# First attention of a four-layer AdaLN/attention/FFN kernel: 16-bit products of ones on TensorE ahead of its waits, and 31 of them in the prologue

## What is computed

```
g  = sigmoid(x) * num / den            # num, den: forward and backward decaying scans of exp(side)
w  = (g @ W.T) as 16 heads of 16       # per sequence
q, k, v = rms(w)*g1, rms(w)*g2, rms(w)*g3
att   = q @ k.T / 4
score = softmax(att, rows) + softmax(att, columns)
x  = x + (score @ v) @ W
```

## Time and profile before

| what | value |
|---|---|
| median of 3 runs | 415.5 us (414.92 to 419.83) |
| the profiled execution, its own time | 418.61 us |
| its span, first to last instruction | 416.8 us |
| mean granted TensorE clock over the span | 0.763 |
| busy: PE, DVE, ACT, POOL | 66%, 71%, 50%, 9% of the span |
| the first attention in this trace | about 36 to 165 us |

### The profile page before, as it was taken

How to read it: one execution, slowest core, us unless ns; L and a number is a source line. 1 busy time by engine, 2 the same in 40 slices (tenths; PEclk the granted TensorE clock), 3 DMA queues, 4 the chain that set the end, 5 groups by cost and what they waited for, 6 DMA issues and landing times.

```text
span 416.8 us, 5215 instructions
## 1 busy us (share of the span) xinstructions
PE 276.7 (66%) x1862; PEld 156.8 (38%) x1867; DVE 296.4 (71%) x536; ACT 208.2 (50%) x422; POOL 39.1 (9%) x61
## 2 busy tenths in 40 slices
PE   0133737548539666637856777979899797975655
PEld 0122314224314224315422245536564454543533
DVE  3998999898798985774598689784436626246861
ACT  5615794865875954352242417415337254332621
POOL 4110120200120113000010100100000000000000
PEclk9999656856957758985785589688658689696985
DMA  7100234445234252005023514391000000000001
GB/s 228 62 0 1 53 68 83 77 76 153 52 69 83 57 102 45 1 1 101 2 50 69 108 31 82 65 267 37 2 0 2 0 2 0 2 0 2 25 25 52
DMA packets 8089, 22.22 MB, mean 53 GB/s; under 512 B 1536, under 2 KB 2944, under 8 KB 7680
## 3 DMA queue, kind: packets, MB, share of 16 engines
q0 software_dynamic: 4032, 14.68, 18.7%
q1 hardware_dynamic: 4032, 7.21, 5.2%
HBM read 6.16 MB, written 1.05 MB: 17 GB/s over the span
## 4 chain that ended last, share of the span: by engine, by line
PE 37%; DVE 36%; issue 11%; ACT 10%; DMA 4%; POOL 0%; DVEq 0%; ACTq 0%; POOLq 0%
DVE fwd L656 5%; PE PS L1222 5%; PE PM L1105 5%; PE PS L1112 4%; PE PO L1238 3%; PE PM L1053 3%; DVE kp L885 3%; PE PM L1175 2%; DVE bwd L662 2%; PE PM L1166 2%; DMA fwd<-mid 2%; DMA fwd<-bwd 2%; ACT E L498 2%; DVE rsum L759 2%; PE PS L1284 2%
## 5 line engine op out<-in xcount | busy, mean ns | idle before, releaser
L885 DVE TENSOR_REDUCE kp<-PS 128x2 f32<-128x256 f32 x64 | 32.3, 550 | 21.0 <-PE PS L1199 20.9
L576 ACT ACTIVATE E<-PS 128x384 f32<-128x384 f32 x64 | 27.8, 488 | 32.7 <-PE PS L1222 32.6
L1112 PE MATMUL PS<-identb 128*128 128x512 bf16 x86 | 33.4, 479 | 16.1 <-ACT E L576 8.4
L498 ACT ACTIVATE E<-PS,negc,escale 128x256 f32<-128x256 f32 x64 | 35.3, 569 | 6.9 <-PE PS L1067 6.9
L1080 PE MATMUL PO<-E,vt 128*32 128x256 f32 x256 | 24.9, 524 | 12.5 <-DVE ytok L787 8.8
L1053 PE MATMUL PM<-ident,kp 128*128 128x128 f32 x128 | 24.4, 353 | 12.9 <-DVE kp L702 7.6
L1088 PE MATMUL PO<-ident,yc 128*128 128x128 f32 x64 | 17.7, 369 | 19.5 <-ACT yc L473 19.5
L490 ACT ACTIVATE E<-PS,negc,escale 128x1024 f32<-128x1024 f32 x16 | 19.2, 1201 | 21.2 <-PE PS L1067 21.2
L1067 PE MATMUL PS<-TP 32*128 32x256 f16 x256 | 21.3, 343 | 9.4 <-DVE TP L714 6.1
L1041 PE MATMUL PM<-w,sg 128*128 128x256 f32 x32 | 12.8, 571 | 21.0 <-DVE sg L689 21.0
L1053 PEld LDWEIGHTS PM<-ident,kp 128*128 128x128 f32 x128 | 19.4, 182 | 18.2 <-issue 9.0
(11 more groups left out here) (179 smaller groups left out, 609.8 us busy)
## 6 DMA issues: line engine op xcount, KB each, us to landing
fwd<-mid POOLq DMA_DIRECT2D x14, 512.0 KB, 4.5
fwd<-bwd POOLq DMA_DIRECT2D x14, 512.0 KB, 4.5
kT<-in_kT SPq DMA_DIRECT2D x4, 256.0 KB, 4.3
xT<-in_xT SPq DMA_DIRECT2D x4, 256.0 KB, 5.8
G<-in_attn SPq DMA_DIRECT2D x1, 1024.0 KB, 4.9
ek<-in_w SPq DMA_DIRECT2D x1, 1024.0 KB, 5.2
ekv<-in_w SPq DMA_DIRECT2D x1, 1024.0 KB, 9.6
out<-mid SPq DMA_DIRECT2D x8, 128.0 KB, 1.7
```

The source lines that it names most:

```text
L498: nc.scalar.activation(E[:, p % 4, i, v * T:(v + 1) * T], PS[:, 2 + i, v * T:(v + 1) * T], ACT.Exp, bias=negc[:], scale=escale[:], accum_o ...
L576: nc.scalar.activation(E[:, p % 4, i, 0:384], PS[:, i, 0:384], ACT.Exp, scale=QSCALE).then_inc(S["e1_done"], 1)
L885: nc.vector.tensor_reduce(kp[:, b % 2, u * H + 2 * j:u * H + 2 * j + 2, D], PS[:, at0:at0 + 2, lo:hi], AX, ALU.max, negate=True).then_inc( ...
L1112: nc.tensor.matmul(bank, identb[:], identb[:, None, :].broadcast_to([P, 4, P]), start=True, stop=True)
```

## The change

`ones` is set to 1.0 at the head of GpSimd's stream, with a semaphore of its own (`ones_set`), instead of behind the two clears of kp. `hot` is a 16-bit view of half of it, and takes the identity's place in all calls of `heat` (those after the first attention too). In the prologue TensorE waits for `ones_set` and for the first scan, and issues 15 products into PS bank 0 ahead of `project0(0)`, 8 behind it, and 8 behind `turn(0)`. In the slots, `warm0(p)` issues one product ahead of `scores0(p)`: at j = 7, and for b >= 1 at j = 0 and 1, into PM bank 0; at j = 2 and 3, for b = 0 also j = 1, for b = 3 also j = 4 and 5, into PM bank 1. That is 4, 5, 5 and 7 products for the four sequences, 21 in all. Each stands behind waits that keep the bank from being overwritten too early, and these now stand ahead of `scores0(p)`.

```diff
+        hot = ones[:, 0:P // 2].bitcast(BF16)
...
+            nc.gpsimd.memset(ones[:], 1.0).then_inc(S["ones_set"], 1)
             nc.gpsimd.memset(lnmin[:], 2.0 ** -60).then_inc(S["ln_bias"], 1)
...
-            nc.gpsimd.memset(ones[:], 1.0).then_inc(S["pads_set"], 1)
             pool.wait_ge(S["gains_done"], 1)
...
-                    nc.tensor.matmul(bank, identb[:], identb[:, None, :].broadcast_to([P, 4, P]), start=True, stop=True)
-
+                    nc.tensor.matmul(bank, hot, hot[:, None, :].broadcast_to([P, 4, P]), start=True, stop=True)
+
+            def warm0(p):
+                b, j = divmod(p, PAIRS)
+                if j == 7 or (j in (0, 1) and b >= 1):
+                    bank = 0
+                    if b < B - 1:
+                        pe.wait_ge(S["qT0_done"], 2 * min(b + 1 + (j == 7), B))
+                    else:
+                        pe.wait_ge(S["qT0_done"], 2 * B)
+                    if p > (B - 1) * PAIRS:
+                        pe.wait_ge(S["w8_done"], 1)
+                elif p > 0 and (j < 4 or (b == B - 1 and j < 6)):
+                    bank = 1
+                    if b >= 2:
+                        pe.wait_ge(S["x_done"], b - 1)
+                else:
+                    return
+                heat(PM[:, bank, :], 1)
+
+            pe.wait_ge(S["ones_set"], 1)
+            pe.wait_ge(S["scan_done"], 1)
+            heat(PS[:, 0, :], 15)
             project0(0)
+            heat(PS[:, 0, :], 8)
             pe.wait_ge(S["ld_ident"], 16)
             turn(0, 0, "ktr0_done", [("k0_done", 1)])
+            heat(PS[:, 0, :], 8)
             for p in range(SLOTS0):
                 b, j = divmod(p, PAIRS)
                 if p < B * PAIRS:
+                    warm0(p)
                     scores0(p)
...
-                    pe.wait_ge(S["pads_set"], 4)
+                    pe.wait_ge(S["ones_set"], 1)
```

More of the change, by code:

```diff
@@ L57 @@
     "gains_done", "ln_bias","qk0_done", "e0_done", "sums_done", "pv0_done", "y0_done", "ytr0_done", "yT0_done",
-    "out0_done", "vcols_done", "rows0_done", "turned0_done",
+    "out0_done", "vcols_done", "ones_set", "rows0_done", "turned0_done",
     "amax_done", "w8max_done", "w8bc_done", "w8_done", "xmax_done", "xbc_done", "xq8_done", "ffn0_done", "y8_done",
```

## The result

| kernel | median, us | against before | 95% interval |
|---|---|---|---|
| changed, first timing (4 runs; before 415.21) | 420.07 | 1.0111 | 1.0057 to 1.0164 |
| changed, timed again (12 runs; before 414.41) | 417.37 | 1.0074 | 1.0040 to 1.0109 |

The change makes the kernel 0.7 to 1.1% slower: 3 to 5 us, under the 2% line, but outside the noise. The first timing is over the 419.5 that ended my range; the longer one lies inside it, but over the 413.5 to 417 of the case that I held likeliest. The profiled execution took 420.28 us, its span is 418.5 us. Ratios here leave out the runs that took over 1.5% more than the fastest of the same kernel, and the profiled executions of five kernels (before, slots alone, added waits alone, slot 7's wait, idle stretches again) were such runs.

What follows compares the result with a forecast made beforehand. VectorE was taken to set the pace, TensorE's clock giving back only VectorE's idle time. Terms 0 + 0.2 - 0.9 - 0.4 - 0.3 + 1.1 = -0.3 us, from a median of 415.5 to 415.2; range 411.5 to 419.5.

Steps and rivals of the forecast that it cites:

- the case that I held likeliest: The prediction's own sum, 415.2 us, range 413.5 to 417; chance 0.42, shared with a rival that nothing is seen.
- GpSimd and prologue: Early clear of `ones` and 31 prologue products: cost 0, gain 0; at most 1 us if the last 8 ran late.
- The wait at slot 25: `scores0(25)` behind `w8_done` delays ScalarE's E to E(27), then VectorE's L767: +1.1 us to the end, at most 2.1.
- The wait at slot 7: `scores0(7)` behind `qT0_done` 4: `values0(2)` 1.0 us late at 1.2 GHz; idle place at 75.41 us taken as +0.2.
- Pairs of scores: A product divides paired score slots; for slots 16 and 17 covered at 2.4 GHz, "just so" at 1.2 GHz.
- The clock and the products in line: Higher clock less products in line: -0.9 us around `project_out(0)`, -0.4 around `project_out(1)`.
- The last `project_out`: `project_out(3)`, near 167.75 us: a gain of 0 to 0.58 us from the clock, taken as -0.3.
- rivals A and C: A: clock stays up, 412.4 us, chance 0.28. C: clock unchanged, products in line, 420.0 us, chance 0.12.
- rival B: The moved waits at slots 25 and 7 decide and the time is longer: +2.2, 417.7 us; chance 0.18.
- Rival C: The clock stays as it was and products lie in line: +6.3 us at most, 420.0 us; chance 0.12.
- The later stages: Second attention and FFN: same work at other moments of the clock, counted as 0 within 2 us.

Runs made afterwards that it cites:

- slots alone: The changed kernel without the prologue's products, keeping the slots' 21 products and waits; 1.0063 of the kernel before.
- added waits alone: The changed kernel with only the slots' added waits, no product in slots or prologue; 1.0050 of the kernel before.
- slot 7's wait: The kernel before with one wait more, `scores0(7)` behind `qT0_done` 4, and no product; 0.9996 of the kernel before.
- idle stretches again: Second timing of the kernel before plus 24 products where TensorE idles: 8 in slot 7, 8 each in slots 14 and 22; 0.9873 of before.
- without slots 7 and 25: The changed kernel without product and wait at slots 7 and 25; 19 products and the prologue stay; 1.0025 of the kernel before.
- prologue alone: The changed kernel with prologue products, early clear and new operand, but no product or added wait in the slots; 0.9996 of the kernel before.
- slot 25's wait: The kernel before with one wait more, slot 25 behind `w8_done`, and no product; 1.0026 of the kernel before.
- the pair of experiments that differ in place alone: The kernel before plus three products in each of 8 odd slots, behind the scores (0.9919 of before) or ahead of them (1.0071).
- even slots alone: The changed kernel with products and their waits in even slots only, 9 of the 21; 1.0061 of the kernel before.

## Why the prediction failed

**GpSimd and prologue: right.** Cost 0 and gain 0, shown alone (0.9996).

**The wait at slot 25: right**, mechanism and size. +1.1 with E(27) late; 1.12 and 0.97 us of new idle time were measured, released by E. The ledger's step is +1.44, of which that idle time is 1.12.

**The wait at slot 7: half right.** TensorE waited as computed (the product at 62.23, behind 5.76 us of idle time), and `values0(2)` came at 64.35, 1.09 us late, where I had 1.0. But `ss` of slot 10 wasn't late (-0.17 for my +0.2), and the wait alone costs no time. That was luck of the clock: `project0(2)` took 1.99 us in this profile. With the slots alone and without slots 7 and 25 it took 3.8, and `ss` was 3.39 and 2.14 us late, outside the +1.9 that ended my range.

**Pairs of scores: right at 2.4 GHz.** The divided pair of slots 16 and 17 is covered: `turn_rows` behind it still waits 0.72 us for yc, where it waited 1.55. At 1.2 GHz, where I had "just so", it isn't: in the kernel without slots 7 and 25 the pair of slots 8 and 9 with its products took 2.1 us more than before, and `turn_rows` (68.51) had no wait left.

**The clock and the products in line: wrong, and this is the step that failed.** I took -0.9 us around `project_out(0)` and -0.4 around `project_out(1)`. The ledger of the profile after gives +1.2 (from -0.17 to +1.03) and +0.2 (1.03 to 1.24). `project_out(0)` took 3.78 us, no less than before, so the 1.7 us that I expected from the clock didn't come; and the products of slots 15 to 18 came on top, half ahead of it, half behind. That is the +1.3 that I had worked out for 1.2 GHz and then given little weight. But the upper level would not have given what I took for it either. I had called the products "mostly covered" there, and -1.7 the price. The clock alone does give 1.71 us (prologue alone), but with the products in the slots 0.85 are left: they cost 0.86 us, where I had set next to nothing. The last `project_out` took 3.78 as well: from 2.68 late to 3.42, +0.7 for my -0.3, of which 0.54 is this product's (3.24 before). With slot 25's step (1.24 to 2.68) these make the 3.4 us at the marker.

The reason behind it was a sentence of mine under rivals A and C: that the products go into the long idle stretches, and that most stand where TensorE waits. They don't. In an in-order stream a product "ahead of the wait" of the scores stands behind the waits of the slot before, and `turn_rows`, `values0` and `turn_y` are where TensorE idles. The groups of the kernel before have the idle time ahead of the scores, without slot 0: 3.3 us in 32 slots. That row alone, which the prediction doesn't use, says that 21 products of 0.2 to 0.6 us can't all hide there.

**The rivals.** By its number rival B came nearest: the moved waits decide, 417.7 us, against 417.4 in the longer timing and 420.07 in the first. Its mechanism explains part, so the match is partly luck: slot 25's wait costs about 1 us, slot 7's nothing that was measured, and all waits together 0.5%, of a total of 0.7 to 1.1%, with an interval from 0.03 to 0.97%. Rival C, to which I had given 0.12, is what the profile looks like: the granted clock stays as it was (0.68 and 0.68 from 80 to 165 us) and the products lie in line. Its 420.0 us is that of the first timing, but with terms of up to 6.3 us, of which the ledger has 3.4. What the waits leave comes, as far as the runs show it, with the products ahead of the scores; the pair of experiments that differ in place alone shows that place is what costs, for three products. For one product I timed no such pair. The stretch of the table above gives it 0.86 us, from single traces with the same `project_out(0)`; what a single product costs apart from waits stays within the noise (1.0025 without slots 7 and 25, and 1.0061 with even slots alone, which differ by no more than their intervals).

**The later stages: right between the two profiles, too narrow for others.** I counted them as 0 within 2 us. From the marker to the end of the span they took 249.1 us before, 247.3 after, and 241.6 in the kernel with slot 25's wait, the same work each time but for the operand of `heat`. So of the 3.4 us at the marker, 1.7 are left at the end of the span. The windows from the marker on show the difference in the granted clock (0.77 before and 0.81 with slot 25's wait; 0.79 after):

```profile
167.75:416.80 249.05, 188.02 (x1204) 108.48 (x1207) 154.14 (x318) 99.63 (x171) 10.64 (x14) 0.77 0.18 39
```

```profile
168.96:410.60 241.64, 181.05 (x1209) 104.83 (x1207) 153.93 (x318) 99.61 (x171) 10.61 (x14) 0.81 0.18 40
```

## What to carry to other kernels

On an in-order engine, "ahead of the wait" means behind the wait of the instruction before. List the idle time by the instruction that it stands ahead of, put filler work right ahead of those with the most, and leave in front of it no wait that can hold it up: the same 24 products were worth -0.8% there and +0.7% one line earlier. And a wait that protects filler work is paid by everything behind it, here 1 us at one slot for a bank that another engine read.

## What I had not expected of the hardware

In the kernel without slots 7 and 25 TensorE was busy 10.17 of 10.24 us, and the granted clock was 0.50 throughout: two products, scores and attention values, then `project0`, and only behind that did it rise. In the trace of before it rose at 66.2 us, right behind `values0` and the scores of slots 8 and 9, with TensorE busy 12.97 of the 20.48 us up to there. So the busy time of a profile doesn't tell which level the clock will take.

The clock's ups and downs also fall at different moments from run to run, and that moves what follows the first attention by 5.7 us between the two profiles of after and of slot 25's wait, and by 7.4 against that of before, while the change moves the kernel by 3 to 5. A single profile of each would have given 416.8 against 418.5 us, and 410.6 for a kernel that is no faster: it takes a marker inside the changed stage, and many timed runs, to see an effect of 1%.
